# A gated cross-attention block: groups 0 and 1 in one stretch, and a prologue that transposes the raw context

## The reference

```python
def rmsnorm(x, scale):
    return x * rsqrt(mean(x * x) + 1e-6) * (1 + scale)

xn, mn = rmsnorm(layernorm(x), rms_scale), rmsnorm(ctx, rms_scale)
q = rope(einsum("BTD,NDH->BTNH", xn, q_w), pos=S + t) * 64 ** -0.5      # 4 heads of 64
k, v = rope(einsum("BSD,DH->BSH", mn, k_w)), einsum("BSD,DH->BSH", mn, v_w)  # one kv head
p = softmax(where(mask, q @ k.T, -2.4e38))
x = x + tanh(g_xattn) * einsum("BTNH,NHD->BTD", p @ v, out_w)
h = gelu(layernorm(x) @ ternary(W1).T + b1)                             # 256 -> 1024
x = x + tanh(g_ffn) * (h @ ternary(W2).T + b2)                          # 1024 -> 256
# ternary(w) = clip(round(w / mean(|w|)), -1, 1)
```

## Time and profile before

| | us |
|---|---|
| median of 3 runs (346.23 to 348.87) | 347.42 |
| the profiled execution: its time | 346.31 |
| its span, first to last instruction | 344.4 |
| TensorE busy in the span | 311.7 (91%) |
| VectorE busy | 256.4 (74%) |
| ScalarE busy | 232.5 (68%) |
| POOL busy | 127.0 (37%) |
| mean granted TensorE clock | 0.97 of 2.4 GHz |

### The profile page before, as it was taken

One profiled execution on the slowest core, in us unless ns is written; L12 is line 12 of the kernel. 1 busy time (PEld: TensorE's weight loads), 2 busy tenths in 40 slices (PEclk: granted clock), 3 DMA queues, 4 the chain that ended last, 5 costly groups with the idle time before them and its releaser, 6 DMA issues.

```text
span 344.4 us, 6831 instructions
## 1 busy us (share of the span) xinstructions
PE 311.7 (91%) x2175; PEld 285.4 (83%) x2175; DVE 256.4 (74%) x825; ACT 232.5 (68%) x595; POOL 127.0 (37%) x151
## 2 busy tenths in 40 slices
PE   8299649766699999999999999999999999999996
PEld 8297539655599988998899988998899889988976
DVE  0567884998559986988698869986998697858443
ACT  0144793337597579757975797579758985896492
POOL 8231237954510363036303540353136313630300
PEclk9769998998799999999999999999999999999999
DMA  6943000020000110011002100110011000100101
GB/s 127 284 129 122 2 0 2 0 64 1 0 2 0 64 47 17 0 63 48 17 0 61 46 15 0 61 46 15 0 64 46 18 0 2 47 17 2 46 16 63
DMA packets 12983, 13.35 MB, mean 39 GB/s; under 512 B 1781, under 2 KB 12397, under 8 KB 12957
## 3 DMA queue, kind: packets, MB, share of 16 engines
q1 hardware_dynamic: 11004, 11.52, 10.4%
q10 hardware_dynamic: 1824, 1.30, 1.5%
q0 software_dynamic: 128, 0.21, 0.8%
HBM read 8.83 MB, written 4.19 MB: 38 GB/s over the span
## 4 chain that ended last, share of the span: by engine, by line
PE 64%; DVE 21%; issue 4%; POOL 4%; ACT 3%; DMA 2%; SPq 0%; DVEq 0%; POOLq 0%
PE ps_m L928 18%; PE ps_h L928 17%; PE ps_m L1113 10%; PE ps_s L928 5%; PE ps_t L936 4%; PE ps_t L1062 3%; DVE s_neg L765 3%; DMA w_raw<-in_ctx_tail 2%; POOL hT_lo L446 2%; DVE s_neg L763 2%; DVE q_sin L708 2%; DVE s_min L769 1%; DVE q_cos L705 1%; DVE x1nT_lo L650 1%; DVE pT_lo L650 1%
## 5 line engine op out<-in xcount | busy, mean ns | idle before, releaser
L406 POOL TENSOR_TENSOR prob<-prob,p_inv 128x512 f32<-128x512 f32 x32 | 33.4, 1044 | 72.4 <-DVE p_inv L773 72.4
L377 POOL TENSOR_TENSOR q_cos<-q_cos,q_sin 128x256 f32<-128x256 f32 x32 | 23.5, 735 | 97.6 <-DVE q_sin L708 97.6
L928 PE MATMUL ps_h<-x1nT_hi,w_tern 128*128 128x512 f32 x128 | 55.0, 429 | 3.1 <-DVE vw_lo L732 2.6
L526 ACT ACTIVATE prob<-s_neg,s_min 128x154 f32<-128x154 f32 x128 | 52.5, 414 | 5.8 <-DVE s_min L769 4.9
L1113 PE MATMUL ps_m<-w_tern,hT_hi 128*128 128x256 f32 x224 | 55.3, 285 | 0.7 <-DVE x_both L796 0.2
L1113 PE MATMUL ps_m<-w_tern,hT_lo 128*128 128x256 f32 x224 | 54.7, 282 | 0.0
L928 PE MATMUL ps_h<-x1nT_lo,w_tern 128*128 128x512 f32 x128 | 51.3, 401 | 0.0
L824 DVE TENSOR_TENSOR hT_lo<-h_all,hT_hi 128x512 fp32r<-128x512 f32 x64 | 42.0, 691 | 8.8 <-ACT hT_hi L557 8.8
L557 ACT ACTIVATE h_all<-ps_h,b_sb 128x512 f32<-128x512 f32 x64 | 45.6, 712 | 3.2 <-PE ps_h L928 2.2
L928 PE MATMUL ps_m<-vw_hi,pT_hi 128*128 128x256 f32 (+1 forms) x160 | 46.7, 292 | 0.0
L557 ACT ACTIVATE hT_hi<-ps_h,b_sb 128x512 fp32r<-128x512 f32 x64 | 45.7, 714 | 0.0
(11 more groups left out here) (136 smaller groups left out, 802.4 us busy)
## 6 DMA issues: line engine op xcount, KB each, us to landing
x_sb<-in_x SPq DMA_DIRECT2D x8, 512.0 KB, 3.6
out_x<-x_both SPq DMA_DIRECT2D x8, 384.0 KB, 2.5
h_all<-in_w1t SPq DMA_DIRECT2D x1, 1024.0 KB, 13.7
w_raw<-in_w2t SPq DMA_DIRECT2D x1, 1024.0 KB, 5.4
out_x<-x_both SPq DMA_DIRECT2D x8, 128.0 KB, 1.7
w_raw<-in_ctx_main SPq DMA_DIRECT2D x1, 512.0 KB
wo_raw<-in_wo ACTq DMA_DIRECT2D x2, 256.0 KB, 10.2
x_both<-in_wq ACTq DMA_DIRECT2D x1, 256.0 KB, 10.7
```

Of the source, the lines that this page charges most:

```text
L377: pool.tensor_tensor(q, q, swapped, ALU.add).then_inc(q_roped, 1)
L406: pool.tensor_tensor(main, main, inv.to_broadcast([P, H, P]), ALU.mult)
L526: e = nc.scalar.activation(prob[t][:, h, :], s_neg[t % 2][:, h, :], ACT.Exp, bias=s_min[t % 2][:, h:h + 1], scale=-1.0, accum_out=p_sum[:, ...
L928: m = pe.matmul(dst, lhs, rhs, start=(n == 0), stop=(n == len(pairs) - 1))
```

## The change

Three things are changed; what is computed stays.

1. **The prologue.** The raw context is transposed as soon as it is there; its rows are de-interleaved (`p (c k) -> p k c`), so that the weights' rows 2p and 2p + 1 lie in one partition. 1 + rms_scale is applied when ScalarE copies the transposed context out of PSUM. The row norms are multiplied into the rotary tables of k (POOL), and together with the gate into the copies of V Wo (`gate_r`, for the tail rows by a small matmul with `tail_sel`). rms_scale and the gates are loaded as rows of one partition and spread over the partitions by five matmuls. Key and value weights are loaded once, unscaled; the value weights are doubled by ScalarE. Buffers are lent from other places, W2 has its home to itself, and SP starts W1's and W2's loads early, ahead of x of group 1. W1, W2 and b1 have semaphores of their own.
2. **Groups 0 and 1** are no longer two steps but one function `fill` on each engine, with one order written out, in which the work of both groups (`FIRST`, `SECOND`), the 12 products V Wo and the ternary pieces are interleaved. `FILL_T`, `FILL_M` and `FILL_H` list its bank uses.
3. **The loop's order.** `T_ORDER`, `M_ORDER` and the steps of all engines are reordered: of x's two transposes for the next group one moves to the front, the third query product comes ahead of the first feed-forward output, the statistics of the next group move back on VectorE, and attention products stand between feed-forward inputs.

The diff, cut to its core:

```diff
-        T_ORDER = ("q0", "q1", "q2", "x1n0", "q3", "x1n1", "p0", "tail0", "p1", "tail1", "xT0", "xT1",
-                   "p2", "tail2", "p3", "tail3")
-        M_ORDER = ("q1", "q2", "y0", "q3", "y1", "y2", "y3", "att0", "att1", "next_q0", "att2", "att3")
+        BEFORE, FIRST, SECOND = Step(-1, 1, -1), Step(0, 0, 0), Step(1, 1, 0)
+        FILL_T = (("xT0", -1), ("xT1", -1), ("q0", 0), ("q1", 0), ("xT0", 0), ("xT1", 0), ("q2", 0), ("q3", 0),
+                  ("tail0", 0), ("p0", 0), ("q0", 1), ("p1", 0), ("q1", 1), ("tail1", 0), ("q2", 1), ("p2", 0),
+                  ("tail2", 0), ("tail3", 0), ("p3", 0), ("p0", 1), ("tail0", 1), ("q3", 1), ("tail1", 1),
+                  ("p1", 1), ("x1n0", 1), ("x1n1", 1), ("xT0", 1), ("xT1", 1), ("tail2", 1), ("p2", 1), ("p3", 1),
+                  ("tail3", 1))
+        FILL_M = (("next_q0", -1), ("q1", 0), ("q2", 0), ("q3", 0), ("next_q0", 0), ("q1", 1), ("q2", 1),
+                  ("att0", 0), ("att1", 0), ("q3", 1), ("att2", 0), ("att3", 0), ("att0", 1), ("att1", 1),
+                  ("next_q0", 1), ("att2", 1), ("att3", 1))
+        FILL_H = (0, 1, 2, "total", 3, 4, 5, 6, 7, 8, 9, 10, 11)
+        CTX_T = ("tail", 0, 1)
+        T_ORDER = ("q0", "q1", "q2", "xT0", "q3", "x1n0", "x1n1", "p0", "tail0", "p1", "tail1", "xT1", "p2",
+                   "tail2", "p3", "tail3")
+        M_ORDER = ("q1", "q2", "q3", "y0", "y1", "y2", "y3", "att0", "att1", "next_q0", "att2", "att3")
...
+            sp.dma_start(w_raw[0][:].rearrange("p (k f) -> p k f", k=KD),
+                         w1t.rearrange("(k p) f -> p k f", p=P)).then_inc(w1_in, 16)
+            sp.dma_start(w_raw[1][:].rearrange("p (k f) -> p k f", k=NF),
+                         w2t.rearrange("(k p) d -> p k d", p=P)).then_inc(w2_in, 16)
             sp.dma_start(x_sb[1][:], x_g[1]).then_inc(x_in[1], 16)
-            sp.dma_start(b1_sb[:], b1).then_inc(w_in, 16)
-            sp.dma_start(w_raw[0][:].rearrange("p (k f) -> p k f", k=KD),
-                         w1t.rearrange("(k p) f -> p k f", p=P)).then_inc(w_in, 16)
-            sp.wait_ge(v_filled, 2)
-            sp.wait_ge(kT_filled, 2)
-            sp.dma_start(w_raw[1][:].rearrange("p (k f) -> p k f", k=NF),
-                         w2t.rearrange("(k p) d -> p k d", p=P)).then_inc(w_in, 16)
-            def step(i, p, b):
...
+            def scale_tables():
+                pool.wait_ge(tab_in, 32)
+                pool.wait_ge(ctx_rstd, 1)
+                r_cos = ctx_r[:].rearrange("p (t c) -> p t c", c=1).to_broadcast([P, CT, C // 2])
+                r_sin = ctx_r[:].rearrange("p (t c) -> p t c", c=1).to_broadcast([P, CT, C])
+                sin = rk_sin[:].rearrange("p t j c -> p t (j c)")
+                pool.tensor_tensor(rk_cos[:], rk_cos[:], r_cos, ALU.mult).then_inc(tab_scaled, 1)
+                pool.tensor_tensor(sin, sin, r_sin, ALU.mult).then_inc(tab_scaled, 1)
...
+            def vw_rounded(n):
+                if n == 0:
+                    act.wait_ge(gate_r_set, 2)
+                act.wait_ge(vw_filled, n + 1)
+                dst, cols = vw_slot(vw_hi, *VW[n])
+                nc.scalar.activation(dst, h_bank(n)[:, cols], ACT.Copy, scale=vw_gate(*VW[n])).then_inc(vw_hi_set, 1)
...
+            def fill():
+                context_rstd()
+                scale_tables()
+                rstd1(BEFORE)
+                wo_rest()
+                rope_add_first(BEFORE)
+                rope_add(FIRST, 1)
+                rope_add(FIRST, 2)
+                tail_values()
+                rope_add(FIRST, 3)
+                rstd1(FIRST)
+                normalise(FIRST, 0)
+                rope_add_first(FIRST)
+                w_low_piece(0)
+                normalise(FIRST, 1)
+                rope_add(SECOND, 1)
+                w_low_piece(1)
+                normalise(FIRST, 2)
+                rope_add(SECOND, 2)
+                w_low_piece(2)
+                normalise(FIRST, 3)
+                w_low_piece(3)
+                normalise(SECOND, 0)
+                w_low_piece(4)
+                w_low_piece(5)
+                rope_add(SECOND, 3)
+                normalise(SECOND, 1)
+                rstd2(SECOND)
+                normalise(SECOND, 2)
+                add_b2(SECOND)
+                w_low_piece(6)
+                w_low_piece(7)
+                normalise(SECOND, 3)
+                rstd1(SECOND)
+                rope_add_first(SECOND)
...
+            def spread_scales():
+                pe.wait_ge(const_set, 2)
+                pe.wait_ge(rows_in, 32)
+                pe.wait_ge(rows_paired, 1)
+                for k in range(KD):
+                    pe.matmul(ps_m[1][:, 2 * k:2 * k + 2],
+                              scale_pairs[:, k].rearrange("o h q -> o (h q)"), ones_sb[0:1, 0:2],
+                              start=True, stop=True)
+                for k in range(KD):
+                    pe.matmul(ps_m[1][:, 2 * KD + 2 * k:2 * KD + 2 * k + 2],
+                              scale_row.rearrange("o (p k) -> o k p", k=KD)[:, k], ones_sb[0:1, 0:2],
+                              start=True, stop=True)
+                pe.matmul(ps_m[1][:, 8:10], ones_sb[0:1, :], gate_row[:], start=True, stop=True).then_inc(rows_spread, 1)
...
+            def fill():
+                pe.wait_ge(const_set, 2)
+                keep_warm(5)
+                spread_scales()
+                keep_warm(5)
+                context_tail_T()
+                context_T(0)
+                context_T(1)
+                keep_warm(2)
+                x_T(BEFORE, 0)
+                x_T(BEFORE, 1)
+                sum_wq()
+                k_products()
+                tail_norms()
+                v_products(0)
+                v_products(1)
+                keep_warm(4, ps_s[1])
+                q_first(BEFORE)
+                keep_warm(4, ps_s[1])
+                k_T()
+                q(FIRST, 1)
+                keep_warm(5)
+                q_T(FIRST, 0)
+                q(FIRST, 2)
+                q_T(FIRST, 1)
+                scores(FIRST, 0)
+                q(FIRST, 3)
+                vw_product(0)
+                x_T(FIRST, 0)
+                x_T(FIRST, 1)
+                scores(FIRST, 1)
+                vw_product(1)
+                q_T(FIRST, 2)
+                q_T(FIRST, 3)
+                q_first(FIRST)
+                vw_product(2)
+                tail_T(FIRST, 0)
+                p_T(FIRST, 0)
+                total_weights()
+                scores(FIRST, 2)
+                q(SECOND, 1)
...
+                q_T(s, 0)
+                q(s, 1)
+                q(s, 2)
+                scores(s, 0)
+                q(s, 3)
+                q_T(s, 1)
+                ffn_out(s, 0)
+                q_T(s, 2)
+                x_T(s, 0)
+                scores(s, 1)
+                ffn_out(s, 1)
+                scores(s, 2)
+                q_T(s, 3)
+                x1_T(s, 0)
+                ffn_out(s, 2)
+                scores(s, 3)
+                x1_T(s, 1)
+                p_T(s, 0)
+                ffn_out(s, 3)
+                tail_T(s, 0)
+                ffn_in(s, 0)
+                p_T(s, 1)
+                ffn_in(s, 1)
+                tail_T(s, 1)
+                attend(s, 0)
+                x_T(s, 1)
+                ffn_in(s, 2)
+                p_T(s, 2)
+                ffn_in(s, 3)
+                attend(s, 1)
+                tail_T(s, 2)
+                ffn_in(s, 4)
+                ffn_in(s, 5)
+                q_first(s)
+                p_T(s, 3)
+                tail_T(s, 3)
+                ffn_in(s, 6)
...
```

1670 lines of the change are left out of this document (980 added, 690 removed).

## The result

The changed kernel takes 316.15 us (median of 4 runs, 315.67 to 316.35), the kernel before 346.85 (4 runs, 346.23 to 348.87): ratio 0.9104, 95% interval 0.9062 to 0.9145. The forecast was 321, with a range of 311 to 331. The profiled execution took 316.32 us with a span of 314.5.

What follows compares the result with a forecast made beforehand. TensorE bounds the loop, chains of hand-overs the stretch of groups 0 and 1, one chain through all engines the prologue. 346.3 - 8.0 - 14.6 - 3.6 = 320.1 us, given as 321 for a median; range 311 to 331.

Steps and rivals of the forecast that it cites:

- rival 1: Whole kernel packs to the floor: stretch of groups 0 and 1 62.0 us, prologue gains 9.0, loop 1.2 per step; 312.5; chance 0.18.
- Part 1, the prologue: Before the first query rotation: transposing the raw context, with norms off the path, gains 8.0 us, bounds 4.3 to 9.0.
- the walk: Prologue steps on TensorE: transposes from 10.6, done 14.6, sum to 16.4, keys 18.8, values 21.1, query product 22.2; 9.0 earlier.
- the 4.3 end of the range: Prologue: keys and values, now 5 us sooner, both run at 1.2 GHz and cost up to 4.7 us more.
- the mark: End of the prologue: the first rotation of a query near 23 us would show the forecast right.
- The rule that was weighed: VectorE and GpSimd lock a shared port pair for whole instructions: at most 5 us more, sum 325; the forecast left it out.
- Part 2, the stretch: Groups 0 and 1, interleaved: VectorE's 62.0 us floor plus 3 us of waits, 65.0 for 79.6; gain 14.6, bounds 17.6 and 0.
- Part 3, the loop: Groups 2 to 7: the new order gains 0.6 us per step, 3.6 over six; bounds 1.2 gained to 0.6 lost each.
- 2: The stretch of groups 0 and 1 does not pack: it takes 75.1 us, a gain of 4.5; total 330.2; chance 0.17.
- 3: The loop loses: early xT0 or the third query product stalls TensorE 0.6 us per step; total 327.3; chance 0.12.
- 4, x of group 1 late: Early stretch: x of group 1, queued behind W1 and W2, lands up to 3 us late; total 323.1; chance 0.05.
- 5, the clock: Stretch of groups 0 and 1: short bursts leave TensorE at 1.2 GHz, 23.2 us longer than the old; total 357.9; chance 0.03.

Runs made afterwards that it cites:

- the first experiment: The changed kernel with GpSimd's rest of the output weights moved behind the second rotary add, from ahead of the first: 315.17 us, ratio 0.9093 to the kernel before.

## Why the prediction was right, and where it was off

**Direction, size and range** were right: 26.2 us were forecast off the span, 29.9 came. The three terms missed by -1.4, +2.9 and +2.1 us, so part of the misses cancelled. In time, 316.15 is 4.9 under the forecast and 3.7 over rival 1 (312.5): the stretch took rival 1's 62.0, the loop's gain is nearer to its 1.2 per step than to 0.6, and it is mostly the prologue, 2.4 us short of rival 1's 9.0, that kept the total from it.

**Part 1, the prologue** (8.0 forecast, 6.6 measured). For TensorE the walk held to within 0.4 us from the end of the column sum on. Two misses ahead of that offset each other: it left out the ten filler matmuls ahead of the transposes and the four between those of context and x, so that the column sum started at 15.33 in place of 14.6; and it priced the sum at the low clock, while the clock was full (1.03 in place of 1.8). That the walk then fits to 0.4 us is in part luck. The fear that keys and values would run at 1.2 GHz (the 4.3 end of the range) did not come true. What failed is that the walk ended with the query product on TensorE. It did not ask what stands ahead of the rotation on VectorE: the sums of the rotated keys beside GpSimd, 2.1 us longer than the 0.89 that they took in the kernel before. Moved apart, the rotation comes at 22.99, near the 23 that was named as the mark. That the norms left the path of the transposes is read from the rows; no run puts them back.

**The rule that was weighed.** The prediction set the rule aside with the sentence that no row shows a wide instruction of VectorE so lengthened. A row for it was there, or likely: the cast of 1.67 in the earlier trace rows, beside a GpSimd subtraction of 2.35. After the change the first 128x320 sum of rotated keys took 2.61 in place of 0.48, and ended 0.35 after GpSimd's instruction did, about its own usual length; apart from it the pair took 0.90. The Trainium skill, "SBUF — State Buffer", section "Who interferes with whom", describes an exclusive lock for a whole instruction, and among what contends it names a VectorE instruction with two SBUF inputs beside a GpSimd instruction that reads SBUF. The sums of the rotated keys are of that form, and for them the trace agrees; the prediction's list of affected forms had left it out. The section frees a VectorE instruction with at most one SBUF input outside the fast two-port modes, and here too the trace agrees: in the first experiment's kernel four statistics over x in SBUF took 1.40 beside the same GpSimd instruction, as without it, and a rest from PSUM 0.42. The ternary pieces, whose two large inputs both lie in SBUF, follow it only in part. In the kernel before one took its usual 0.74 inside a GpSimd comparison (from 61.02); in the kernel with the rotary add moved two took 1.17 and 0.95 beside the same comparisons. And in the changed kernel it can be GpSimd that pays, here a normalisation that began just behind a ternary piece and took 1.46 in place of 1.04:

```profile
50.15 0.72 DVE L907 SCALAR_TENSOR_TENSOR w_tern<-h_all,w_thr,hT_lo 128x512 fp32r<-128x512 f32 x1
```

```profile
50.31 1.46 POOL L457 TENSOR_TENSOR prob<-prob,p_inv 128x512 f32<-128x512 f32 x1 [0.81 <-DVE p_inv L1008]
```

The stretch, which the prediction's reading of the rule would have made slower by up to 5 us, was not: VectorE's work in it fell from 62.0 to 59.9.

**Part 2, the stretch** (14.6 forecast, 17.5 measured). The mechanism was right and the allowance was mis-sized: 3 us for VectorE's waits, of which 2.15 came, while the floor of 62.0 fell by 2.1 itself. Three variances took 0.51 in place of 2.22, with GpSimd quiet beside them; one shift (`mr`) that does meet it took 1.00 in place of 0.15. Another 1.2 did not vanish but left the stretch: the mask conversion (0.5) now stands ahead of the first rotation, and one rest of a GELU (0.7) behind the last attention product. That is rival 1 in this stretch. The chain piece of GpSimd in the earlier trace rows was named as the largest single one; put back, it costs 6.8 of the 17.5. The one opening of it that was tried in the old kernel, a single rotary add ahead of four of the six comparisons, gave nothing. That the spreading is worth something only with the two groups in one order is likely but not shown, and no run prices the other 10.7 us.

**Part 3, the loop** (3.6 forecast, 5.7 measured). 1.08 per step in place of 0.6. The variance was rightly named; with its statistics and power it is 0.45 in the old order. The rest of the new order, which the forecast mentioned and gave no number of its own, is the other 0.6. The x load, of which it said that only 0.5 us was left, is not late: TensorE shows no wait for it between 90 and 258 us.

**Rivals.** 2 and 3 did not happen. 4, x of group 1 late: VectorE takes it at 28.42 with no wait. 5, the clock: it stayed at 1.00 in the changed kernel. In the kernels made from it the mean over the span was 0.994 or more, but for the one with the comparisons in one row (0.988 to 0.995). The Trainium skill, "TensorE: Matmul & The Clock Gate", section "HAM oscillation — how this bites in real kernels", tells of a kernel whose engine falls back at every wait for a transfer, waits that are longer than the work between them. The prediction took that as a rule for any wait, and the trace does not bear it out: the longest wait of TensorE in the new stretch was 1.76 us (at 68.29) and no spell followed. The wait of 5.03 us in the kernel with the comparisons in one row was followed by 0.50 from 63 to 66 us. As far as these traces show, rival 5 would have needed longer waits than the new order leaves.

## What to carry to other kernels

When you walk a chain by engines, end it with the instruction that reads the result, and look through that engine's own queue, and at what GpSimd runs beside it. A wide GpSimd instruction over SBUF was better placed, in the one case tried, where VectorE reads PSUM or runs statistics. Take each block of filler matmuls out once the order is settled: of the four taken out here one had cost 1.6 us, two 0.8 together and one nothing in the median. Look at the clock of every execution then, not only of the profiled one: without the last block it was below full in two of six. And price a change of order in the order where it will stand: the late statistics were worth 0.45 per step in the old loop and 0.90 in the new one.
